# A 13x13 depthwise convolution on TensorE with 15 instead of 18 matmuls a channel

## The reference

```python
# layer 0: attention over channels, on a grid of 96 x 96
qkv = einsum(gn(x), w_qkv) + b_qkv          # 1x1 convolution, 384 -> 1152
qkv = max over 2x2; qkv = depthwise 3x3(qkv) + b_dw
# 8 heads of 48 channels: four top-k softmaxes of q k^T, times v, gelu
x = x + upsample 2x(out) @ w_proj + b_proj
# layer 1
y = gn(x)
x = x + bn_l(depthwise 13x13(y)) + bn_s(depthwise 3x3(y)) + bn_i(y)
```

## Time and profile before

| | us |
|---|---|
| timed runs, median of 3 (range) | 3048.57 (3047.66 to 3050.59) |
| profiled execution, own time | 3045.88 |
| its span | 3044.2 |
| PE busy in the span | 2745.2 (90%) |
| DVE busy | 2435.4 (80%) |
| ACT busy | 1382.1 (45%) |
| POOL busy | 29.0 (1%) |
| mean granted TensorE clock | 0.981 |

### The profile page before, as it was taken

How to read it: one execution, slowest core, us unless ns; L and a number is a source line. 1 busy time by engine, 2 the same in 40 slices (tenths; PEclk the granted TensorE clock), 3 DMA queues, 4 the chain that set the end, 5 groups by cost and what they waited for, 6 DMA issues and landing times. The chain is left out here.

```text
span 3044.2 us, 51281 instructions
## 1 busy us (share of the span) xinstructions
PE 2745.2 (90%) x18425; PEld 2007.7 (66%) x18425; DVE 2435.4 (80%) x3319; ACT 1382.1 (45%) x1729; POOL 29.0 (1%) x46
## 2 busy tenths in 40 slices
PE   0059999999999999999968999948999999999998
PEld 0036666666666666666645666637999999999997
DVE  7958999999999999999987898947565566666563
ACT  0044445555555555544224777745444444444442
POOL 0010000000000000000000000000000000000000
PEclk9999999999999999999989999969999999999999
DMA  9964111111111111110027999959988988999986
GB/s 336 416 212 150 49 64 62 65 66 62 66 67 60 66 68 59 66 61 16 16 75 236 340 344 345 348 169 281 288 281 281 282 272 279 278 286 279 286 248 186
DMA packets 228823, 564.24 MB, mean 185 GB/s; under 512 B 29248, under 2 KB 134464, under 8 KB 225600
## 3 DMA queue, kind: packets, MB, share of 16 engines
q1 hardware_dynamic: 211392, 495.41, 50.7%
q10 hardware_dynamic: 17280, 66.85, 5.8%
HBM read 402.21 MB, written 159.99 MB: 185 GB/s over the span
## 5 line engine op out<-in xcount | busy, mean ns | idle before, releaser
L1510 PE MATMUL cv_cb<-cv_hi,cv_toep 128*128 128x288 f16 (+1 forms) x4608 | 909.9, 290 | 31.6 <-DVE cv_lo L1444 28.8
L743 PE MATMUL qk_qb<-qk_xhi,whi 128*128 128x384 f16 x2592 | 846.9, 327 | 20.7 <-DVE qk_xlo L639 14.3
L743 PE MATMUL qk_qb<-qk_xlo,whi 128*128 128x384 f16 x2592 | 846.8, 327 | 0.0
L743 PE MATMUL qk_qb<-qk_xhi,wlo 128*128 128x384 f16 x2592 | 846.7, 327 | 0.0
L660 DVE SCALAR_TENSOR_TENSOR qk_dw<-qk_pool,qk_wd,qk_dw 128x768 f32<-128x768 f32 (+2 forms) x864 | 836.6, 1009 | 2.5 <-ACT qk_dw L528 2.4
L1510 PE MATMUL cv_cb<-cv_lo,cv_toep 128*128 128x288 f16 (+1 forms) x2304 | 667.6, 290 | 0.0
L1510 PEld LDWEIGHTS cv_cb<-cv_hi,cv_toep 128*128 128x128 f16 x4608 | 522.6, 113 | 91.7 <-DVE cv_lo L1444 28.9
L647 DVE TENSOR_REDUCE qk_pool<-qk_qb 128x192 f32<-128x768 f32 x432 | 412.0, 954 | 69.4 <-PE qk_qb L743 53.2
L1398 ACT ACTIVATE cv_res<-cv_cb,cv_cst 128x288 f32<-128x288 f32 x384 | 191.9, 501 | 555.3 <-PE cv_cb L1510 555.3
L1456 DVE COPY cv_rows<-cv_bb 128x512 f32<-128x512 f32 x216 | 145.7, 686 | 323.3 <-PE cv_bb L1491 323.3
L743 PEld LDWEIGHTS qk_qb<-qk_xhi,whi 128*128 128x128 f16 x2592 | 254.1, 98 | 184.3 <-DVE qk_xlo L639 17.8
(11 more groups left out here) (150 smaller groups left out, 2284.2 us busy)
## 6 DMA issues: line engine op xcount, KB each, us to landing
cv_toep<-toeplitz_scratch SPq DMA_DIRECT2D x384, 384.0 KB, 4.8
patch_scratch<-pr_turned SPq DMA_DIRECT2D x75, 832.0 KB, 9.5
cv_raw<-patch_scratch SPq DMA_DIRECT2D x24, 2600.0 KB, 10.7
st_x<-in_x SPq DMA_DIRECT2D x24, 2304.0 KB, 17.1
qk_xf<-in_x SPq DMA_DIRECT2D x72, 768.0 KB, 4.2
pr_xb<-in_x SPq DMA_DIRECT2D x24, 2304.0 KB, 10.0
...
```

The lines of the kernel that those rows point to most:

```text
L743: ins = nc.tensor.matmul(qbank[s % NQB][:, h, 0:2 * W], w[:, b, o * P:(o + 1) * P], x[:, par, j // 2, b, at_row:at_row + 2 * W], start=n = ...
L1510: ins = nc.tensor.matmul(out, toep[:, c % NTOEP, :].rearrange("p (s m v) -> p s v m", s=NS, m=P)[:, s, u * 2 + part], x[:, par, c, u:u + O ...
```

## The change

The last shift down, `s` = 2, reaches only the upper half of the rows of a patch: 13 taps from 8 rows of pixels end in the fourth row of the third patch. Before, its table was half empty, in its input rows as in its output rows. Now:

- The pixels of a patch are reordered over the partitions: partitions 0 to 63 hold rows 0 to 3 of the patch, 64 to 127 rows 4 to 7. So the raw patches and the taps are loaded as two transfers of 64 partitions each (`load_group`, `load_taps`).
- For `s` = 2 the two shifts across are joined: `hi_last` and `lo_last` hold the upper halves of the patches for `u` = 0 in partitions 0 to 63 and for `u` = 1 in 64 to 127, and one table `late` of 128 x 64 multiplies both. Six matmuls become three, with 64 output partitions. The tables `late` are built in the qkv stage (POOL copies, SP stores in packets of 256 bytes) and loaded four channels at a time (`load_late`).
- The `s` = 1 matmuls read copies, `hi_next` and `lo_next`, which are shifted by one patch and have no gaps between rows of 24. DVE makes these and `lo_last`; ACT makes `hi_last`.
- `hi` and `lo` and all copies have one buffer instead of two, so a piece of the next group is split only after the same piece of this group is convolved. DVE normalises into a new buffer `norm` (two pieces) in the order that `hi` and `lo` have; the border masks are two instructions instead of four.
- The order on DVE and ACT is written anew.

```diff
-NS, NU = 3, 2
+NS, NU = 2, 2
+HALF_ROWS = TH // 2
+HP = P // 2
...
+                if inner:
+                    for ix in (t * 2 - 4, t * 2 - 3):
+                        for b in range(CB):
+                            address(sp, ix * (HALF_ROWS * ERUN), 2)
+                            sp.wait_ge(late_made, ix * (2 * CB) + 2 * b + 2)
+                            for u in range(NU):
+                                windows = bass.AP(late, (b * NU + u) * EROWS * TW * 2,
+                                                  [[CB * NU * EROWS * TW * 2, P], [TW * 2, HALF_ROWS], [1, ERUN]])
+                                sp.dma_start(edge_dram[b * P:(b + 1) * P, u, bass.ds(ix, 1), :, :]
+                                             .rearrange("p a y n -> p (a y) n"), windows).then_inc(late_out[b], 16)
...
+            def late_taps(ix):
+
+                for b in range(CB):
+                    if not at(ix, 0):
+                        gp.wait_ge(late_out[b], ix * (16 * NU))
+                    for part in range(2):
+                        window = bass.AP(padw, (b * 2 + part) * KL * JX + (KL - ETAPS) * JX + ix,
+                                         [[CB * 2 * KL * JX, P], [TW, NU], [JX, ETAPS], [1, TW]])
+                        G.tensor_copy(late[:, b, :, 0:ETAPS, :, part], window).then_inc(late_made, 1)
+
+            late_taps(0)
+            with gp.Fori(1, TW) as ix:
+                late_taps(ix)
...
     def load_group(sp, g, par):
-        sp.dma_start(raw[:, par].rearrange("p i c j -> p (i c j)"),
-                     patch_dram[:, bass.ds(g, 1), :, :].rearrange("p a i n -> p (a i n)")).then_inc(raw_in[par], 16)
+
+        for h in range(2):
+            v = patch_dram[h * HALF_ROWS:h * HALF_ROWS + 1, bass.ds(g, 1), :, :].rearrange("p a i n -> p (a i n)")
+            sp.dma_start(raw[h * HP:(h + 1) * HP, par].rearrange("p i c j -> p (i c j)"),
+                         bass.AP(v.tensor, v.offset, [[TH * PITCH, TW], [PITCH, HALF_ROWS], [1, TI * GRP * TJ]])).then_inc(raw_in[par], 16)
...
+        norm = sb("norm", [P, 2, CPP, TJ, TI])
+        hi = sb("hi", [P, GRP, TJ, TIP], F16)
+        lo = sb("lo", [P, GRP, TJ, TIP], F16)
+        hi_next = sb("hi_next", [P, GRP, TJ, OI], F16)
+        lo_next = sb("lo_next", [P, GRP, TJ, OI], F16)
+        hi_last = sb("hi_last", [P, GRP, OJ, OI], F16)
+        lo_last = sb("lo_last", [P, GRP, OJ, OI], F16)
...
+        def free(eng, g, q):
+
+            if not at(g, 0):
+                eng.wait_ge(conv_done, g * GRP - GRP + (q + 1) * CPP)
...
+            def load_taps(g, c):
+
+                ch = g * GRP + c
+                address(sp, ch * (TW * JR * RUN), 2)
+                if not isinstance(g, int) or ch >= NTOEP:
+                    sp.wait_ge(conv_done, ch - NTOEP + 1)
+                v = toep_dram[bass.ds(ch, 1), :, :].rearrange("a i n -> (a i) n")
+                for h, skip in ((0, SKIP * RUN), (1, 0)):
+                    sp.dma_start(toep[h * HP:(h + 1) * HP, c % NTOEP, skip:KRUN],
+                                 bass.AP(v.tensor, v.offset, [[JR * RUN, TW], [RUN, HALF_ROWS], [1, KRUN - skip]])).then_inc(
+                                     toep_in[c % NTOEP], 16)
+
+            def load_late(g, q):
+
+                first = g * GRP + q * CPP
+                address(sp, first * (P * ERUN), 2)
+                sp.dma_start(late[:, q % NQUAD * CPP:(q % NQUAD + 1) * CPP, :],
+                             edge_dram[bass.ds(first, CPP)].rearrange("c u x y n -> (u x y) c n")).then_inc(
+                                 late_in[q % NQUAD], 16)
...
+            SPLIT_AT = {3: 0, 7: 1, 11: 2}
+            LAST_AT = {4: 0, 8: 1, 12: 2}
...
+            def split(g, q):
+
+                act.wait_ge(edge_done, g * NPC + q + 1)
+                free(act, g, q)
+                nc.scalar.activation(hi[:, part_of(q), :, 0:TI].rearrange("p c j i -> p (c j) i"),
+                                     norm[:, q % 2].rearrange("p c j i -> p (c j) i"), ACT.Copy).then_inc(hi_done, 1)
+
+            def last_high(g, q):
+
+                act.wait_ge(hi_done, g * NPC + q + 1)
+                for u in range(NU):
+                    ins = nc.scalar.activation(hi_last[u * HP:(u + 1) * HP, part_of(q), :, 0:EI],
+                                               hi[0:HP, part_of(q), u:u + OJ, NS:TI], ACT.Copy)
+                ins.then_inc(hi_last_done, 1)
...
-                for c in range(q * CPP, (q + 1) * CPP):
-                    V.tensor_scalar(raw[:, par, :, c, :], raw[:, par, :, c, :],
+                    dve.wait_ge(raw_in[par], (g // 2) * 32 + 32 if isinstance(g, int) else (g - par) * 16 + 32)
+                piece = norm[:, q % 2]
+                for k in range(CPP):
+                    c = q * CPP + k
+                    V.tensor_scalar(piece[:, k].rearrange("p j i -> p i j"), raw[:, par, :, c, :],
                                     cst[:, bass.ds(g * GRP + c, 1), 0], cst[:, bass.ds(g * GRP + c, 1), 1],
                                     ALU.subtract, ALU.mult).then_inc(norm_done, 1)
-                piece = raw[:, par, :, q * CPP:(q + 1) * CPP, :]
                 base = g * (NPC * PARTS) + q * PARTS
                 dve.wait_ge(norm_done, base + CPP)
-                V.tensor_scalar(piece[:, :, :, 0], piece[:, :, :, 0], side[:, 0:1], None, ALU.mult).then_inc(norm_done, 1)
-                V.tensor_scalar(piece[:, :, :, TJ - 1], piece[:, :, :, TJ - 1], side[:, 1:2], None, ALU.mult).then_inc(norm_done, 1)
-                dve.wait_ge(norm_done, base + CPP + 2)
-                V.tensor_scalar(piece[:, 0], piece[:, 0], side[:, 2:3], None, ALU.mult).then_inc(norm_done, 1)
-                V.tensor_scalar(piece[:, TI - 1], piece[:, TI - 1], side[:, 3:4], None, ALU.mult).then_inc(edge_done, 1)
-
-            def low(g, par, q):
+                columns = piece[:, :, 0:TJ:TJ - 1, :]
+                V.tensor_tensor(columns, columns, side[:, 0:2].unsqueeze(1).unsqueeze(3).broadcast_to([P, CPP, 2, TI]),
+                                ALU.mult).then_inc(norm_done, 1)
+                dve.wait_ge(norm_done, base + PARTS)
+                border = piece[:, :, :, 0:TI:TI - 1].rearrange("p c j i -> p (c j) i")
+                V.tensor_tensor(border, border, side[:, 2:4].unsqueeze(1).broadcast_to([P, CPP * TJ, 2]),
+                                ALU.mult).then_inc(edge_done, 1)
+
+            def low(g, q):
                 dve.wait_ge(hi_done, g * NPC + q + 1)
                 dve.wait_ge(edge_done, g * NPC + q + 1)
-                dve.wait_ge(norm_done, g * (NPC * PARTS) + (q + 1) * PARTS)
-                if not (isinstance(g, int) and g < 2):
-                    dve.wait_ge(conv_done, g * GRP - 2 * GRP + (q + 1) * CPP)
-                half = lo[:, par, q * CPP:(q + 1) * CPP, :, 0:TI].rearrange("p c j i -> p (c j) i")
-                V.tensor_tensor(half, raw[:, par, :, q * CPP:(q + 1) * CPP, :].rearrange("p i c j -> p (c j) i"),
-                                hi[:, par, q * CPP:(q + 1) * CPP, :, 0:TI].rearrange("p c j i -> p (c j) i"),
+                V.tensor_tensor(lo[:, part_of(q), :, 0:TI].rearrange("p c j i -> p (c j) i"),
+                                norm[:, q % 2].rearrange("p c j i -> p (c j) i"),
+                                hi[:, part_of(q), :, 0:TI].rearrange("p c j i -> p (c j) i"),
                                 ALU.subtract).then_inc(lo_done, 1)
+
+            def next_rows(g, q):
+
+                V.tensor_copy(hi_next[:, part_of(q)], hi[:, part_of(q), :, 1:1 + OI]).then_inc(hi_next_done, 1)
+                dve.wait_ge(lo_done, g * NPC + q + 1)
+                V.tensor_copy(lo_next[:, part_of(q)], lo[:, part_of(q), :, 1:1 + OI]).then_inc(lo_next_done, 1)
+
+            def last_low(g, q):
+
+                for u in range(NU):
+                    ins = V.tensor_copy(lo_last[u * HP:(u + 1) * HP, part_of(q), :, 0:EI],
+                                        lo[0:HP, part_of(q), u:u + OJ, NS:TI])
+                ins.then_inc(lo_last_done, 1)
...
-            ORDER = ("N0", "B0", "B1", "N1", "B2", "L0", "B3", "N2", "B4", "B5", "L1", "N3", "B6", "B7", "B8", "L2", "L3")
+            split(0, 2)
+            ORDER = ("N0", "L3", "N1", "B0", "B1", "L0", "B2", "N2", "B3", "B4", "L1", "B5", "N3", "B6", "L2", "B7", "B8")
+            FIRST = ("L3",) + tuple(w for w in ORDER if w != "L3")
...
+            def channel(g, c):
+
+                bank = cbank[c % NCB]
+                taps = toep[:, c % NTOEP, :].rearrange("p (s m v) -> p s v m", s=NS, m=P)
+                few = late[:, c % NTOEP, :].rearrange("p (m v) -> p v m", v=2)
+                whole = bank[:, 0:NPIX].rearrange("p (j i) -> p j i", j=OJ)
+                upper = bank[0:HP, 0:NPIX].rearrange("p (j i) -> p j i", j=OJ)[:, :, 0:EI]
+                for u in range(NU):
+                    for k, (part, x) in enumerate(((0, hi), (0, lo), (1, hi))):
+                        nc.tensor.matmul(whole, taps[:, 0, u * 2 + part], x[:, c, u:u + OJ, 0:OI],
```

(54 more changed lines are left out.)

141 lines of the change are left out of this document (73 added, 68 removed).

## The result

The changed kernel takes 3107.39 us (median of 4 runs, 3103.42 to 3108.31) against 3049.58 for the kernel before beside it: ratio 1.0187, 95% interval 1.017 to 1.0205. The forecast was 2901 us with a range of 2878 to 3015. The direction was wrong: 58 us slower instead of 148 faster. The profiled execution took 3103.42 us, its span is 3101.5.

A forecast was written before the change was run, and what follows sets the result against it. TensorE was taken to bound the convolution: 3045.9 us minus 23 groups of 6.8 (156), plus 5 for POOL and 4 for small waits, gives 2898.5; with the timed median 2.7 higher, 2901, range 2878 to 3015.

The forecast's parts named there:

- I take 0.1233 for the three that stay: TensorE, s=2: six matmuls become three, each still 0.1233 us start to start, saving 0.370 us a channel.
- the 0.425 that were counted: TensorE's forecast saving per channel in us, from 2.275 to 1.850: 0.370 from s=2 and 0.055 from s=1.
- Rival D: TensorE: three joined matmuls cost as much as six, as narrow output breaks the rhythm; about 3037 us, chance 0.02.
- Rival B: DMA queue becomes the bound, half-partition transfers at half rate: group 38 us, time 3003 us, chance 0.15.
- the 5 us for POOL: qkv stage: POOL's 96 copies hold VectorE up; bounds 0 and 50 us, taken 5.
- The s=1 term: TensorE: six s=1 matmuls from an even start fall from 0.1325 to 0.1233 us each, 0.055 us a channel.
- The copies, the weakest number: VectorE: four new two-byte copies a piece, taken 0.43 us each on average, 1.7 us a piece.
- A2: VectorE a little too slow, copies 2.6 us a piece: group about 36 us, time 2960 us, chance 0.14.
- C: VectorE copies run at one element a cycle: group 45 us, time 3188 us, slower than before; chance 0.17.
- the byte rate: VectorE copies timed by bytes, from four-byte elements at 1.04 ns each: 0.69 and 0.61 us a copy.
- Single buffers: Split pieces wait for the previous group, 4.5 us plus up to two normalises, wanted after 22 us: cost 0.
- The start: Convolution start: first matmul at 2061.9, TensorE gets four channels each time, group 1 at about 2102; no gain for the first group.

The follow-up runs named there:

- spread_narrow: raw_spread with the joined matmuls 64 output columns wide again, as in the changed kernel: 2976.4 us.
- raw_spread: The changed kernel with cv_late's ring of 16 channels issued 12 ahead, joined matmuls 128 columns wide, raw data in four spread transfers: 2889.0 us.
- late_ahead: The changed kernel with a ring of 16 channels for cv_late, issued 12 channels before use in place of 4: 2994.0 us.
- spread_only: The changed kernel with only the raw load spread, four transfers at channels 2, 5, 8 and 11: 2981.2 us.

## Why the prediction was wrong

**The step that failed** has two parts, both about cv_late: a term that was mis-sized and a wait that the sum did not have.

"I take 0.1233 for the three that stay": they come at 0.12, but the way in and out costs 0.24 us of the 0.425 that were counted. By spread_narrow that is 87 us. Rival D named this mechanism ("narrow output breaks the rhythm") and got 0.02, because I priced it as all or nothing and no row of before had narrow output. It should have been an unknown term with both ends in the range. The Trainium skill, "TensorEngine Tiling (Array Packing)" (Key Properties), states that changing the tiling mode drains TensorE; 128 by 64 is another mode in its list. The 0.21 and 0.22 us between the starts fit it (that they are a drain is not shown), and I did not weigh it.

The other part was missing. The sum never asked when cv_late is *due*. Rival B saw slow half transfers, and its rate, half of 416 GB/s, is what the raw pair ran at: 206. But it took the rate for all loads and as throughput, so many MB in so many us: a group of 38 us at share 1. Measured were 42.8 us at share 0.84, and raw_spread, with the same half transfers, needs 33.4 us a group: throughput was sufficient. What failed was one landing a group: 8.3 us allowed, 12 needed behind 2.6 MB of raw data. Issuing cv_late earlier (late_ahead) removes it, and so does spreading the raw data (spread_only). Its price is 3107 - 2981 = 126 us, of which the waits are 87.9 us (whole span, 22 of them, the last number of this row). The rest is 38 us; the matmuls at 1.2 GHz behind two of the waits cost 2.3 and 1.2 us, by which I estimate 26 to 51 us for 22:

```profile
L1619 PE MATMUL cv_cb<-cv_hi,cv_toep 128*128 128x288 f16 x1536 | 364.3, 297 | 117.7 <-DMA cv_late<-toeplitz_edge_scratch 87.9
```

From raw_spread to the changed kernel the runs make a ladder: 2889 (everything mended) + 87 (width) + 5 (spread_narrow to spread_only, cv_late's short lookahead, within the scatter) + 126 (burst) = 3107. It closes by construction; what it shows is the size of each step.

The slow rate belongs to the burst's price, which I overlooked. From the raw pair's issue to the landing of cv_late the queue has 2.66 MB of raw data, 0.92 of taps and 0.13 of cv_late to move. At 206 GB/s that takes 18.0 us, near the 19.3 measured. At the 354 GB/s of a whole transfer in the kernel before it would take 10.5, and cv_late is due 15.6 us after that issue. By this estimate a raw load to all 128 partitions would have been in time even as a burst; no run tried it.

**What held.** raw_spread runs as the sum described, and it takes 2889 us where the sum said 2901. Its groups take 33.4 us where nothing waits and 33.7 on average, against 33.55 and 4 us of small waits in all; group 1 begins at about 2100.3 instead of 2102 plus the 5 us for POOL, and that is most of the difference. From its trace:

```profile
L1536 DVE TENSOR_SCALAR cv_norm<-cv_raw,cv_cst 128x325 f32<-128x325 f32 x304 | 143.1, 617 | 0.6
```

- Channel: 2402.27 to 2404.11, 1.84 us (1.850 forecast). The s=1 term was 21 us and measured 20.5.
- VectorE: one group, 2403.2 to 2436.7, has 28.4 us of it, against 31.9. The overestimate cost nothing, since TensorE needs more. Four normalises take 1.88 us, 0.47 each where I took 0.63: the write 25 words apart costs less than the nearest row.
- The copies, the weakest number, fell on the taken value, which was a judgement and so partly luck. In the changed kernel

```profile
L1550 DVE COPY cv_lo_last<-cv_lo 64x1104 f16<-64x1104 f16 x130 | 58.8, 452 | 0.9
...
L1543 DVE COPY cv_hi_next<-cv_hi 128x1248 f16<-128x1248 f16 x65 | 32.8, 505 | 0.0
```

  505 ns with the next start 0.42 us later; the four copies of one piece take 1.76 us (2415.57 to 2417.33), taken were 1.7. That kills A2 and C; the byte rate would be 0.69 us a copy.
- ScalarE: 21.2 us in that group, 21 forecast. Single buffers: no wait of TensorE for a split piece in 2200 to 2900 us. POOL: 0.4 us in place of 5. Stores of the edge table: no cost found.
- The start went another way than forecast. TensorE begins at 2056.73, before the forecast 2061.9. It does not stand after every four channels, as the sum had it, but for loads: once for cv_toep and, after eight channels, for cv_late. Group 1 begins at about 2106.5 (first transposes at 2112.74, three channels behind), against 2102.

```profile
2056.73 0.40 PE L1619 MATMUL cv_cb<-cv_hi,cv_toep 128*128 128x288 f16 x1 [27.20 <-DVE cv_lo_last L1550]
...
2066.16 0.43 PE L1619 MATMUL cv_cb<-cv_hi,cv_toep 128*128 128x288 f16 x1 [2.62 <-DMA cv_toep<-toeplitz_scratch]
...
2087.25 0.40 PE L1619 MATMUL cv_cb<-cv_hi,cv_toep 128*128 128x288 f16 x1 [5.55 <-DMA cv_late<-toeplitz_edge_scratch]
```

**Open.** Whether the burst would have done harm with a raw load to all partitions: by the estimate above not, but a whole transfer in the changed kernel's order of partitions wasn't tried. Open is also which part of the 0.24 us is a drain and which a weight load that doesn't run ahead.
